# A hybrid kernel on one core: the first sum of each of the first twelve pieces between scan and attention is written to PSUM instead of SBUF

## What is computed

```python
ys = ys + xs * Ds.reshape(1, K, Di, 1)          # four directions, skip term
y = ys[:, 0] + ys[:, 2, :, ::-1]
y2 = ys[:, 1] + ys[:, 3, :, ::-1]
y = y + y2.reshape(B, Di, Wd, H).transpose(0, 1, 3, 2).reshape(B, Di, L)
y = _ln(y, og, ob); out = y @ out_W             # then + skip_scale * xi
...
y = _ln(concat(outs), ln_g, ln_b) @ proj_W + proj_b
t = t + _L1_attn_ref(_ln_t(t))                   # tokens, L2-normalized
```

## Time and profile before

| | us |
|---|---|
| median of 3 runs (lowest, highest) | 5875.48 (5871.67, 5880.47) |
| the profiled execution, its own time | 5875.91 |
| its span in the profile | 5874.2 |
| busy PE / DVE / ACT / POOL over the span | 5065.8 / 4213.8 / 3787.4 / 4271.6 |

### The profile page before, as it was taken

How to read it: one execution, slowest core, us unless ns; L and a number is a source line. 1 busy time by engine, 2 the same in 40 slices (tenths; PEclk the granted TensorE clock), 3 DMA queues, 4 the chain that set the end, 5 groups by cost and what they waited for, 6 DMA issues and landing times. The chain is left out here.

```text
span 5874.2 us, 82875 instructions
## 1 busy us (share of the span) xinstructions
PE 5065.8 (86%) x21540; PEld 3376.1 (57%) x21540; DVE 4213.8 (72%) x4029; ACT 3787.4 (64%) x8376; POOL 4271.6 (73%) x2720
## 2 busy tenths in 40 slices
PE   4777388998899899889998999897799999995997
PEld 2344255555555555555555555554458888884675
DVE  3677599999999999999999999997751111118334
ACT  2566588888888888888888888885442222226332
POOL 0567699999999899999998999997504444444442
PEclk8888599999999999999999999998999999996998
DMA  3666677777777777777777777777500000004113
GB/s 94 171 198 205 209 235 247 249 246 251 240 246 248 241 247 246 244 248 243 243 249 239 248 245 247 249 248 263 194 23 1 0 0 0 0 0 123 50 58 132
DMA packets 395504, 1045.37 MB, mean 178 GB/s; under 512 B 53422, under 2 KB 90319, under 8 KB 390944
## 3 DMA queue, kind: packets, MB, share of 16 engines
q1 hardware_dynamic: 382464, 1010.05, 54.1%
q0 software_dynamic: 7584, 20.72, 1.1%
q10 hardware_dynamic: 4992, 9.44, 0.4%
HBM read 869.23 MB, written 170.79 MB: 177 GB/s over the span
## 5 line engine op out<-in xcount | busy, mean ns | idle before, releaser
L920 POOL TENSOR_TENSOR scan_hc<-scan_h,scan_c_rep 128x768 f32<-128x768 f32 x1536 | 2749.2, 1821 | 233.9 <-PE scan_ps_y L751 177.2
L751 PE MATMUL scan_ps_y<-scan_hc,keep_ident 128*128 128x512 f32 (+1 forms) x6144 | 2219.8, 489 | 23.4 <-ACT scan_y L786 23.0
L885 DVE TENSOR_TENSOR_SCAN scan_h<-scan_da,scan_h,scan_ps_p 128x768 f32<-128x768 f32 x896 | 1568.7, 1796 | 0.0
L751 PEld LDWEIGHTS scan_ps_y<-scan_hc,keep_ident 128*128 128x128 f32 x6144 | 1067.9, 190 | 824.1 <-issue 739.3
L803 ACT ACTIVATE scan_warm<-scan_du_t 128x128 f32<-128x128 f32 x4608 | 1423.6, 388 | 38.7 <-PE scan_ps_p L742 32.9
L842 ACT ACTIVATE scan_da<-scan_dd,layer_a_neg 128x768 f32<-128x768 f32 x1344 | 1184.8, 922 | 4.4 <-issue 3.6
L1464 POOL TENSOR_TENSOR attn_e_lo<-attn_e,attn_e_hi 128x512 fp32r<-128x512 f32 x324 | 418.1, 1290 | 610.9 <-DVE attn_e_hi L1455 610.9
L742 PE MATMUL scan_ps_p<-keep_ident,scan_warm 128*128 128x128 f32 x4608 | 647.9, 277 | 222.2 <-DVE scan_h L885 221.3
L885 DVE TENSOR_TENSOR_SCAN scan_h<-scan_da,scan_ps_p 128x768 f32<-128x768 f32 x448 | 758.9, 1735 | 2.3 <-ACT scan_da L842 2.0
L742 PEld LDWEIGHTS scan_ps_p<-keep_ident,scan_warm 128*128 128x128 f32 x4608 | 532.7, 141 | 372.2 <-issue 156.9
L864 DVE TENSOR_TENSOR scan_ps_p<-scan_ps_p,scan_dd 128x768 f32<-128x768 f32 x576 | 547.5, 951 | 194.2 <-PE scan_ps_p L734 193.0
(11 more groups left out here) (328 smaller groups left out, 6910.4 us busy)
## 6 DMA issues: line engine op xcount, KB each, us to landing
scan_c_rep<-bc_dram SPq DMA_DIRECT2D x1536, 384.0 KB, 4.2
scan_dd<-dd_dram SPq DMA_DIRECT2D x96, 768.0 KB, 5.7
scan_b_rep<-bc_dram SPq DMA_DIRECT2D x192, 384.0 KB, 4.9
dd_dram<-delta_de SPq DMA_DIRECT2D x96, 384.0 KB, 2.6
dd_dram<-delta_du SPq DMA_DIRECT2D x96, 384.0 KB, 3.2
y_dram<-scan_y SPq DMA_DIRECT2D x96, 384.0 KB, 4.6
mid_nat<-y_dram SPq DMA_DIRECT2D x48, 384.0 KB, 7.8
delta_img<-xn_dram SPq DMA_DIRECT2D x16, 576.0 KB, 8.6
```

What stands on the lines that cost most here:

```text
L751: mm = pe.matmul(ps_y[:, lo:hi], keep["ident"][:, :], hc[t % HR][:, lo:hi], start=n == 0, stop=n == N - 1)
L885: dve.tensor_tensor_scan(view(h[n]), view(x), view(y), start, ALU.mult, ALU.add).then_inc(scan_done, 1)
L920: pool.tensor_tensor(hc[t % HR][:, :], h[t % N][:, :], c_rep[t % CR][:, :], ALU.mult).then_inc(hc_done, 1)
```

## The change

In `join(st)` the destination of the first sum, and with it the first operand of the second, is now chosen by the piece. For st < 12 it is `ps_y` (odd st) or `ps_x` (even st), the first 384 columns of each of its two banks; from piece 12 on it is `a` in SBUF as before. All operands are written as [128, 2, 384] instead of [128, 768]. The semaphores, their counts and the order of instructions on all engines are the same.

```diff
             def join(st):
                 dve.wait_ge(n_done, st + 1)
-                dve.scalar_tensor_tensor(a[st % AR][:, :], nat[st % NR][:, 2, :], d_sum[:, 0:1], a[st % AR][:, :],
-                                         ALU.mult, ALU.add).then_inc(a1_done, 1)
+                v = lambda x: x[:, :].rearrange("p (n t) -> p n t", n=2)
+                part = (ps_y if st % 2 else ps_x)[:, :, 0:TT] if st < HALF else v(a[st % AR])
+                dve.scalar_tensor_tensor(part, v(nat[st % NR][:, 2, :]), d_sum[:, 0:1], v(a[st % AR]), ALU.mult, ALU.add).then_inc(a1_done, 1)
                 dve.wait_ge(a1_done, st + 1)
                 dve.wait_ge(b_done, st + 1)
-                dve.tensor_tensor(a[st % AR][:, :], a[st % AR][:, :], flat(q[st % AR][:, :, :]), ALU.add).then_inc(a_done, 1)
+                dve.tensor_tensor(v(a[st % AR]), part, q[st % AR][:, :, :], ALU.add).then_inc(a_done, 1)
```

## The result

The changed kernel takes 5861.57 us (median of 20 runs, 5853.19 to 5869.97), the kernel before in as many runs 5870.66 us (5860.66 to 5880.47). The ratio is 0.9986 with a 95% interval of 0.998 to 0.9992, that is 4.7 to 11.7 us less. The profiled execution of the change took 5859.48 us, with a span of 5857.6.

The account below looks back on a forecast made before the run. The prediction took a shared line of DVE and POOL instructions, 7.01 us a piece, as the bound in the first half. At 6.2 us, ten pieces save 0.8 each, 8.0 us, giving 5867.5 us, range 5862 to 5874.

Parts of the forecast that it names:

- Within 0.2%: Whole kernel: time staying within 0.2% (11.8 us) of the time before, given 0.84.
- The line of five instructions: First half: L1290, L1277, L1043, L1281, L1038 run one after another, summing to 7.03 us a piece against 7.01 measured.
- (a): Pieces 0 to 11: L1277 writes PSUM, stays in the line, costs 0, bounds 0 to 0.1 us each.
- (b): Pieces 0 to 11: L1281, with one PSUM and one SBUF input, takes 0.96 us and leaves the line.
- The two orders, 5.98 and 6.36: New line period: 5.98 us if L1290 gets between L1043 and L1038, 6.36 if it comes just too late.
- 6.2 us a piece: First half: period taken from limits 5.98 to 6.36, 6.13 and 6.2 us, 0.8 less than before.
- Transfers, 6.13 us a piece at 353 GB/s: First half: full DMA engines need 6.13 us for a piece's 2.163 MB, a limit near the line's.
- the sum: First half: 0.8 us saved on each of pieces 2 to 11, 8.0 us in all.
- Pieces 2 and on give 0.8 each at once: Savings of pieces 0 and 1 are lost at piece 3; pieces 2 to 11 each save 0.8 us.
- the latency as a loop over DVE and two pieces: L1281 to L1182 plus DVE's work spans two pieces: 5.6 us a piece at full clock, limit taken 6.2.
- Rival 2: First half: transfers or half-clock latency replace the line, period only 6.6 to 6.9 us, 1 to 4 us gained; 20%.
- Everything shifts: Second half and after: length unchanged, so all later work moves earlier by what the first half gained.

Follow-up runs that it names:

- r_before: The kernel before, unchanged, executed once more to see how far its stages repeat: first half of the phase 107.3 us.
- dest_only: The changed kernel with L1282 again adding two SBUF inputs, so the first twelve pieces omit the skip term: first half 107.0 us.
- lite_after: The changed kernel without the xs loads from the fifth piece on, adding the stale buffer instead: first half 99.9 us.
- first6: The kernel before with the change applied to pieces 0 to 5 alone: first half 104.4 us.
- skip_last: The changed kernel with ACT's scaling of the skip input moved behind the root in the first half: 5867.86 us, ratio to before 0.998.

## Why the prediction was right, and where it was off

Within 0.2% was the likeliest case and is what came: 8.0 us less were forecast, 9.1 measured by the medians, interval 4.7 to 11.7. The median of 5861.57 us itself is 0.4 under the low end of the range, 5862, which had been set from a median before of 5875.48; over 20 runs that is 5870.66.

- *The line of five instructions sets 7.01 us.* Right: r_before repeats it, and taking a member out shortens it, once to 6.0 to 6.3, twice to 5.3. The account left one thing out: from L1290 to L1043 it is not only the turn at SBUF, L1043 also waits for L1290's `z_done`.
- *(a) the write to PSUM costs 0.* Right: 1.01 to 1.03 us uncontended, 1.01 in dest_only. The Trainium skill, "VectorE: DVE Perf Modes", section "The TRN2 errata — SBUF-src ops pay a fixed extra latency per instruction", charges 62 cycles more for a PSUM source; they do not show: 957 ns from PSUM, 958 from SBUF.
- *(b) L1281 takes 0.96 and leaves the line.* Right, in twelve of twelve.
- *The two orders, 5.98 and 6.36.* Both are there: 6.02 in lite_after, 6.37 between POOL's L1043 of pieces 6 and 7 in the change.
- *6.2 us a piece.* Too short: this is the term that was mis-sized. L1291 of pieces 3 to 11 comes every 6.4, 6.7 and 6.6 us, L1290 before every 7.0. Of 0.8 us a piece 0.5 came on the mean, for the reasons of the next two points.
- *Transfers, 6.13 us a piece at 353 GB/s.* Mis-sized: that rate came from a stretch that began with the first loads; in mid-run full engines give 331 to 339, 6.4 to 6.5 us. From L1043 of piece 5 to that of piece 13 there are 8 pieces, for which the sum had 8 x 0.8 = 6.4 us. Before they took 55.9 and 56.3 us, in the change 50.3, 52.6 and 52.2: a mean gain of 4.4.
- *Pieces 2 and on give 0.8 each at once.* Wrong for the first ones. Up to L1043 of piece 5 the sum had pieces 2 and 3, 1.6 us; measured in the three executions of the change, by whichever two one compares, 0.1 to 1.0, and 2.1 to 2.7 in first6, where the rounds around `ps_c` happened to be short. I had looked for the latency as a loop over DVE and two pieces, and missed PE and ACT around `ps_c`, one piece long (5.8 us at full clock, up to 11.1 here), and ACT's fixed order behind a late `xn`. By skip_last that order costs 2.0 to 3.5 us at piece 5 against the three executions, 0.3 to 1.5 against first6. The second pair of the earlier trace rows, called piece 5, is piece 6; the 6.0 us worked out from it stand.
- *Rival 2, a half-clock latency or transfers take the line's place.* Right in part: its sign, DVE waiting for L1182, is there in ten of the twelve pieces of the first execution of the change.
- *Everything shifts.* Right: second half 243.3 and 244.0 before, 243.1, 243.1 and 244.0 after; POOL's wait for nat at piece 3 grew from 0.42 to 1.6 us, as it had to if the first pieces' gain is lost there.

In the phase the change gives 5.2 us where 8.0 were worked out, and the median shows 9.1. The mechanism was right; that 8.0 comes so near to 9.1 is in part luck, for the sum was 2.8 us too large where it can be looked up. The part that I can place is 5.2 us.

## What to carry to other kernels

If a sum on VectorE takes 3.5 us now and 0.96 at its best, look at GpSimd's timeline beside it: with both inputs in SBUF it stands in GpSimd's line, and an intermediate left in a free PSUM bank takes it out, here at no cost that showed. Add up the members of such a line from end to end before and after; then ask what is second, since a line that was full hid everything else: here full DMA engines at 6.4 us a piece, and an engine's fixed order behind a late load. Where the effect is as small as the scatter of a phase that was not touched, compare lengths of stages over several executions, not two spans.

## What I had not expected of the hardware

- A VectorE instruction that waits gets in at each end of a GpSimd instruction, even when GpSimd's next is ready: in the kernel before, L1281 ended 0.8 us after L1043's end, and L1038, for which no wait is shown, took 2.55 instead of 1.80 us. lite_after has it at both ends: L1279 ended at 4114.26, 0.8 us after L1038 (4110.89 to 4113.44), though L1043 started at 4113.40 without a wait. L1290 in the kernel before is no such case, since L1043 waited for its `z_done`.
- Full DMA engines moved 350 GB/s over the first half (share 1.02) but 331 to 339 over its middle (1.03 and 1.04), and 361 in the 65 us from 4033.55, 3 us after the phase's start (1.03). So at the same share the rate falls by 6% within the phase; why is open. The Trainium skill, "SBUF — State Buffer", section "A bandwidth-pool intuition that's wrong (but worth ruling out)", has about 358 for HBM to a core: the first 65 us reach it, the middle does not.
